# Second product of 64 experts: w2 held still, result turned back, rows eight units ahead

## The reference

```
def _swiglu(x, w1, w2):
    h = x @ w1.T                          # 128 -> 768
    x1, x2 = jnp.split(h, 2, axis=-1)
    return x1 * jax.nn.silu(x2) @ w2.T    # 384 -> 128
x = x + 0.5 * _L0_ffn_ref(_layernorm(x), wg, shared_w1, shared_w2, expert_w1, expert_w2)
x = x + _L0_attn_ref(_layernorm(x), ...)
x = x + 0.5 * _L0_ffn_ref(_layernorm(x), wg, shared_w1, shared_w2, expert_w1, expert_w2)
```

## Time and profile before

| | |
|---|---|
| median of 3 runs | 3281.57 us (3281.53 to 3283.92) |
| profiled execution, span from first to last instruction | 3607.6 us (its own time: only this span is given) |
| granted TensorE clock (share of full), mean over the span | 0.854 |
| TensorE busy | 2593.0 us, 72% |
| GpSimd busy | 1846.4 us, 51% |
| VectorE busy | 2038.9 us, 57% |
| ScalarE busy | 1370.6 us, 38% |
| table adds of stage one, first to last | 364.2 to 590.8 us |
| table adds of stage two, first to last | 1067.8 to 1292.5 us |

### The profile page before, as it was taken

The page is one execution under the profiler, slowest core; times in us unless marked ns, Lnnn a source line. Parts: engine busy times, 40 slices in busy tenths (PEclk is TensorE's granted clock), DMA queues, the critical chain, the costliest instruction groups (busy, mean ns, idle before and its releaser), DMA issues. The chain is left out here.

```text
span 3607.6 us, 68811 instructions
## 1 busy us (share of the span) xinstructions
PE 2593.0 (72%) x24634; PEld 1681.5 (47%) x24634; DVE 2038.9 (57%) x5864; ACT 1370.6 (38%) x2937; POOL 1846.4 (51%) x2072
## 2 busy tenths in 40 slices
PE   1224994735499945689998899947388886999573
PEld 1113884423368834356555555536133332555362
DVE  4347334523443345547885587621699999787413
ACT  1111221301122222344665266622576763466323
POOL 5650775254317742126996213456488886123554
PEclk7666997856599977799999799978699999899786
DMA  9100896121019974331110101112221211111123
GB/s 373 48 1 8 213 224 155 45 66 31 27 41 226 226 191 108 138 120 21 19 19 3 20 19 30 48 55 56 102 94 48 94 62 40 22 20 35 43 80 92
DMA packets 222721, 294.13 MB, mean 82 GB/s; under 512 B 36704, under 2 KB 179583, under 8 KB 216288
## 3 DMA queue, kind: packets, MB, share of 16 engines
q1 hardware_dynamic: 172704, 249.85, 22.3%
q0 software_dynamic: 47616, 39.44, 5.8%
q10 hardware_dynamic: 2112, 1.05, 0.1%
HBM read 181.88 MB, written 107.12 MB: 80 GB/s over the span
## 5 line engine op out<-in xcount | busy, mean ns | idle before, releaser
L3783 POOL TENSOR_TENSOR l3am_db<-l3am_du,l3am_bs 128x1024 f32<-128x1024 f32 x127 | 298.0, 2367 | 39.9 <-DVE l3am_hh L4021 36.1
L4021 DVE TENSOR_TENSOR_SCAN l3am_hh<-l3am_dA,l3am_db 128x1024 f32<-128x1024 f32 x128 | 292.1, 2283 | 0.9 <-ACT l3am_dA L3921 0.7
L1217 POOL TENSOR_TENSOR l2a_pT<-l2a_pT,kept 128x512 int32<-128x512 int32 x213 | 265.1, 1280 | 45.4 <-ACT l2a_pT L1423 45.4
L3066 POOL DMA_INDIRECT l0f_table<-l0f2e_y,l0f2e_idx x128 | 178.9, 1398 | 177.1 <-DVE l0f2e_idx L3038 130.2
L3066 POOL DMA_INDIRECT l0f_table<-l0f1e_y,l0f1e_idx x128 | 179.6, 1403 | 139.2 <-DVE l0f1e_idx L3038 91.2
L4152 PE MATMUL l3am_y<-l3am_hc,ident 128*128 128x512 f32 x512 | 242.1, 596 | 0.0
L3921 ACT ACTIVATE l3am_dA<-l3am_dl,l3am_al 128x512 f32<-128x512 f32 x256 | 166.3, 682 | 130.8 <-DVE l3am_hh L4021 127.2
L1894 POOL DMA_INDIRECT l0f_rows<-l0f1r_row,l0f1r_idx x160 | 159.7, 998 | 103.1 <-issue 69.3
L1304 DVE CUSTOM_DVE_ANT_0 l2a_junk<-l2a_s,addend 128x256 f32<-128x256 f32 x486 | 178.1, 421 | 57.0 <-PE l2a_s L1540 44.6
L1297 DVE TENSOR_REDUCE l3f1a_mx<-l3f1a_s 128x2 f32<-128x512 f32 x243 | 156.5, 685 | 40.9 <-PE l3f1a_s L1540 32.4
L1297 DVE TENSOR_REDUCE l3f2a_mx<-l3f2a_s 128x2 f32<-128x512 f32 x243 | 156.4, 684 | 39.7 <-PE l3f2a_s L1540 32.1
(11 more groups left out here) (848 smaller groups left out, 7045.5 us busy)
## 6 DMA issues: line engine op xcount, KB each, us to landing
l3am_bs<-l3a_b SPq DMA_DIRECT2D x32, 1024.0 KB, 6.6
l0f1m_w<-in_L_ffn_expert_w SPq DMA_DIRECT2D x64, 384.0 KB
l0f2m_w<-in_L_ffn_expert_w SPq DMA_DIRECT2D x64, 384.0 KB
l1a_top<-l1a_kernel SPq DMA_DIRECT2D x16, 1024.0 KB, 12.6
l0f_rows<-blank SPq DMA_DIRECT2D x8, 1930.0 KB, 15.2
l0f1m_w<-in_L_ffn_expert_w SPq DMA_DIRECT2D x64, 192.0 KB
l0f2m_w<-in_L_ffn_expert_w SPq DMA_DIRECT2D x64, 192.0 KB
l3f_rows<-blank SPq DMA_DIRECT2D x8, 1440.0 KB, 11.6
```

The source lines that it names most:

```text
L1217: self.nc.gpsimd.tensor_tensor(t, t, self.kept[:, f // 8 % 2, :].unsqueeze(1).to_broadcast([P, 2, 2 * P]), ALU.mult).then_inc(self.cut_g, 1)
L3066: g.indirect_dma_start(out=tables[p], out_offset=bass.IndirectOffsetOnAxis(ap=idx[u % RING][:, a:a + 1], axis=0), in_=y[u % RING][:, a, :] ...
L3783: G.tensor_tensor(db[n % DB][:, :].rearrange("p (j t) -> p j t", j=CC), du[k % 2][:, :, :], bs[s // QUARTER][:, s % QUARTER, :].unsqueeze( ...
L4021: V.tensor_tensor_scan(hh[n % HH][:, :], dA[n % 2][:, :], db[n % DB][:, :], 0.0, ALU.mult, ALU.add).then_inc(h_ready, 1)
```

## The change

Both 64-expert stages call a new function, `gated_experts`, instead of `experts`; the 8-expert stages keep the old one. It differs in this:

- The second product keeps w2 stationary (128 columns) and moves the 160 gated columns, three products in all; the result is features by places, 128x160. ACT copies it to SBUF (`oT`), and TensorE turns it back in two transposes into the other half of the same PSUM bank (`back`).
- TensorE's step is `output(n)`, first half of `hidden(n+2)`, `back(n)`, second half of `hidden(n+2)`, `turn(n+3)`: one unit deeper than before.
- ACT's and DVE's steps run one unit deeper too; the silu and the gating product are those of unit n+1.
- There are 8 row buffers and the programs are written 8 units at a time; rows are loaded 8 units ahead, after y of unit n; the weights are still 4 ahead, but are issued after `output(n)`, not after y.
- y waits for `back(n)`. Ring of 4 y buffers, two tables, and POOL's program stay.

```diff
+def gated_experts(nc, c, name, w, m, mats, E, C1, KC, A):
+    rows, tables, sub, V, PLACES, RING = m.rows, m.tables, SUB, 8, mats.places, 4
...
+        row = [ph.sb(f"row{i}", [sub, A, R]) for i in range(V)]
+        oT = [ph.sb(f"oT{i}", [P, S]) for i in range(2)]
...
+        @block.sync
+            def step(at):
+                i, u, n = at(0)
+                if at(PLACES):
+                    sp.wait_ge(o_done, n + 1)
+                    mats.load(sp, at(PLACES)[2], u % PLACES)
+                if at(V):
+                    sp.wait_ge(y_ready, n + 1)
+                    load_rows(at(V)[2], u)
+            for u in range(V):
+                load_rows(u, u)
+            stream(sp, units, V, step)
...
+            def output(i, u, n):
+                p = u % 2
+                pe.wait_ge(g_ready, n + 1)
+                if not isinstance(n, int) or n >= 2:
+                    pe.wait_ge(y_ready, n - 1)
+                for f in range(KC):
+                    mm = nc.tensor.matmul(ob[p][:, 0:S], mats.t2[u % PLACES][:, f, :], gT[p][:, f * S:(f + 1) * S],
+                                          start=(f == 0), stop=(f == KC - 1))
+                mm.then_inc(o_done, 1)
+            def back(i, u, n):
+                p = u % 2
+                pe.wait_ge(oT_ready, n + 1)
+                for a in range(A):
+                    mm = nc.tensor.transpose(ob[p][0:sub, (2 + a) * D:(3 + a) * D], oT[p][:, a * sub:(a + 1) * sub],
+                                             c.ident[:, :])
+                mm.then_inc(back_done, 1)
+            def step(at):
+                output(*at(0))
+                if at(2):
+                    hidden(*at(2), 0)
+                back(*at(0))
+                if at(2):
+                    hidden(*at(2), 1)
+                if at(3):
+                    turn(*at(3))
...
+            def result(i, u, n):
+                a_.wait_ge(o_done, n + 1)
+                nc.scalar.activation(oT[u % 2][:, :], ob[u % 2][:, 0:S], ACT.Copy).then_inc(oT_ready, 1)
+            def step(at):
+                if at(1):
+                    bend(*at(1))
+                result(*at(0))
+                if at(3):
+                    copy(*at(3))
...
+            def step(at):
+                i, u, n = at(0)
+                p = u % 2
+                if at(1):
+                    gate(*at(1))
+                if not isinstance(n, int) or n >= RING:
+                    v.wait_ge(added[p], 16 * A * ((V // 2) * i + (u - RING) // 2 + 1))
...
+                v.wait_ge(back_done, n + 1)
+                nc.vector.tensor_tensor(y[u % RING][:, :, :],
...
-        experts(nc, c, name + "e", w, m, mats, 64, 6, 3, 2, True)
+        gated_experts(nc, c, name + "e", w, m, mats, 64, 6, 3, 2)
```

96 lines of the change are left out of this document (95 added, 1 removed).

## The result

The changed kernel takes 3321.57 us (3314.92 to 3326.63, four runs) against 3281.55 (3277.50 to 3283.92, four runs): slower, ratio 1.012 with a 95% interval of 1.0101 to 1.0138, or +40 us. Of this, 34 us lie between the first and the last table add of the two stages.

A forecast was written before the change was run, and what follows sets the result against it. GpSimd was taken as the bound, 3.41 us a unit. y in time -4.5, landings -2.1 and later first y +1.2 gave -5.4 us, scaled by 0.91 to -4.9: 3276.7 us, range 3252 to 3291.

The forecast's parts named there:

- What bounds the kernel: 64-expert stages: GpSimd's two table adds need at least 3.41 us a unit, against 3.09 for TensorE's own step.
- The second product: TensorE's step falls 0.25 us to 2.84; the first y comes 0.57 us later, +1.2 us over two stages.
- The rows: Row loads eight units ahead: TensorE's 27.3 us of row waits go; y in time gains 4.5 us.
- Landings: GpSimd's waits for earlier adds to land, 8.2 us: a quarter gained, -2.1 us.
- the 4.5 that I had put for y: GpSimd's waits for a late y: 0.8 us sure plus 3.7 of the open 7.4, gained.
- Rival 3: Adds waiting for those of two units before: landings get worse, half the units hit, +15 us, 3297 us; chance 0.13.
- Rival 1: TensorE or the rows bind in the runs, not GpSimd: up to -30 us, 3257 us; chance 0.22.
- The clock: TensorE's clock might fall with four turns a unit and idle time; nothing in the sum; as a rival 3550 us, chance 0.02.
- Code: Unrolled loop bodies grow from four units to eight: cost zero, upper bound 5 us.
- the fill: Start of each stage: the first y comes 0.57 us later, +1.2 us for two stages.

The follow-up runs named there:

- y2: Changed kernel with w1 transfers bringing 256 of 768 columns, all instructions, waits and order kept; ratio to before 0.9968, adds 435.0 us in both stages.
- x3: Changed kernel with the old second product, no copy and no turns back, rows still eight ahead; ratio to before 1.0086, adds 477.6 us.
- z1: Changed kernel with the weights issued after y of unit n, not after its second product; ratio to before 1.0086, adds 485.7 us.
- x2: Kernel before with the new second product, copy and turns back, but still four row buffers and weights after y; ratio to before 1.0150, adds 498.1 us.
- x1: Kernel before, unchanged, profiled once more on chip 7; adds 227.2 and 226.1 us, whole program 3608.98 us.
- y4: Changed kernel with weights of unit n+4 also held until GpSimd's program is between the two adds of unit n-1; ratio to before 1.0111, adds 512.1 us.

## Why the prediction was wrong

- **What bounds the kernel** was right: GpSimd's 3.41 us a unit, not TensorE, though TensorE shows the higher busy share. y2 ran at that floor (435.0 us; the floor of both stages was put at 216.4 + 215.5 = 431.9).
- **The second product**: step of 2.84 us, turns back 0.22 (0.24 predicted), copy hidden. Right, and worth nothing by itself as long as GpSimd is the bound. The 0.57 us by which the first y was to come later can't be read: from the first turn of a stage to its first y, profiles of before took 8.0 to 11.1 us and those of the changed kernel 8.7 to 11.7.
- **The rows**: TensorE's 27.3 us of waits for them went, and y was no longer late. Right; GpSimd's waits under "issue" fell from 7.4 us, after 0.30 us each and without the two stops of 3.0 together, to 3.4.
- **Landings: this step failed.** I had the mechanism down as "once y runs ahead it waits for the landing of the adds of four units before, and the bursts lock to that", and, beside it, that weights and rows now leave apart and their bursts are spread; then I took a quarter of 8.2 us as *gained*, a term of -2.1 us. The runs show a loss, and bursts in pairs instead of spread ones. Off GpSimd's landing waits, after 0.30 us each: 30.6 - 24 x 0.30 = 23.4 us in stage one and 31.4 - 7.2 = 24.2 in stage two, 47.6 together against 8.2. This term measured +39 us for my -2.1; less the 4.5 that I had put for y, some 35 remain, and the adds show 34.
- **Rival 3** named place and sign and half of the mechanism (y ahead, held by landings; not that two units' bursts leave together), and had 0.13 and 3297 us. Its price was mis-sized in one factor: I took 0.44 us a hit unit from the waits of before; in the rhythm a hit costs 23.4 / 24 = 0.98 us. The number of units hit was about right, 48 of 128 with the label of a landing where I had 64. 48 x 0.98 = 47 us for my 28.
- **Why so small a chance?** I argued from the first profile that phases differ along a stage and only few units are hit. But before, TensorE was held by rows, and each burst left after a y that had waited for them: w1 issues were mostly 3.3 to 3.8 us apart, and none under 2. With rows ahead of time nothing spaced them any more: x3 and z1 have 27 and 29 close issues, x2, with the rows as before, none. "The bytes do not change" was no comfort: the share fell and the landings came later all the same.
- **Rival 1** (0.22, and the lower part of the range) rested on the 10% between profile and runs. x1 shows the expert stages unchanged in a profile of 3618 us, so the 10% had nothing to say about them. It should have had far less.
- **The clock**: the prediction had "a clock under 1.00" as a sign of being wrong and nothing in its sum. The granted clock was 0.94 and 0.97 over the two stages, before 0.99 and 1.00. It fell after TensorE had idled for 2 us:

```profile
440.50 1.48 PE L3154 MATMUL l0f1e_o<-l0f1e_gT,l0f1m_w 128*128 128x160 f32 x6 [2.08 <-DVE l0f1e_gT L3215]
```

  The same product takes 1.02 us at full clock, and the half hidden layer behind it, at 441.78, took 1.81 us for 0.98: that is the lower of the two levels, 1.2 GHz. No wait of GpSimd near it is ended by y, so no cost can be seen. The rule of the Trainium skill ("TensorE: Matmul & The Clock Gate", Part 4: a transpose in transpose mode does not count as busy in the same way) can't be told from this: with four turns a unit the clock was 1.00 in most windows, also in 360 to 380, and no run changes the turns alone without the waits.
- **Code**: nothing in the waits points to the longer loop bodies, and over stage one the larger code queue moved four transfers for three before; it wasn't tried by itself.
- 40 us in all less 34 between the adds leaves some 6 for the fill (about 1) and the rest of the kernel. Its place stays open; the runs of one kernel in one place differ by that much and more (3314.92 to 3326.63).

What stays open as well: how long an add lands behind one burst and behind two was not measured by itself, and the exact order of packets on the transfer engines was not followed. That it is the transfers is shown (y2); that it is their coming in pairs rests on the count of close issues over the runs and on the lines of y4, not on a run that changes the spacing and nothing else.

## What to carry to other kernels

A wait that hides on an engine with slack may be what spaces the transfers of a neighbour. Before removing it, ask which engine now runs ahead, what it will wait for next, and which transfers that releases together; the average load on the transfer engines does not answer that. When one engine is the bound by its own issue time, pace the others' bulk transfers by it, and then look in the trace at when they really leave: the place of a semaphore in the program doesn't tell.

## What the runs showed of the hardware

The same program took 3282 us where the result was taken and 3607 to 3622 us on chips 7, 4 and 9, with the same duration in these stages (226.6 and 227.2 us in stage one): a profile and a time are only compared when they come from one place. A semaphore raised in GpSimd's program after an add took effect up to 1.8 us before the add began in the trace (y4). Transfer engines at a share of 0.78 over the stage delayed adds more than at 0.87, when w1 issues came two by two, 1.6 us apart and then 6; with 441 of 697 KB a unit the adds ran at GpSimd's floor of 3.41 us a unit.
